# A second copy of the context in 32x32 squares, transposed in place by VectorE, instead of TensorE's context transposes

## What is computed

```python
h = _lin(_layernorm(x), hW, hb);  c = _lin(ctx_1024, cW, cb)
q = _lin(h, qW, qb);  k = _lin(c, kW, kb);  v = _lin(c, vW, vb)
attn = softmax(einsum('bqf,bkf->bqk', q, k) * scale)      # 512 queries x 8192 keys, per batch
x = x + _lin(einsum('bqk,bkf->bqf', attn, v) + q, oW, ob)
x = x + ssm_layer(_layernorm(x))      # layernorm, in_w, convolution with a 16-term kernel, silu gate, out_w
x = x + chosen_expert(_layernorm(x))  # argmax of 8 gates, one 512x512 matrix per token
```

## Time and profile before

| what | value |
|---|---|
| median of 3 runs | 1283.13 us (1282.91 to 1284.45) |
| the profiled execution's own time | 1280.48 us |
| its span, first to last instruction | 1278.8 us |
| TensorE matmul busy | 1203.6 us, 94% |
| VectorE busy | 910.0 us, 71% |
| ScalarE busy | 493.8 us, 39% |
| GpSimd busy | 327.9 us, 26% |
| mean granted TensorE clock | 0.977 of full speed |

### The profile page before, as it was taken

The page is one execution under the profiler, slowest core; times in us unless marked ns, Lnnn a source line. Parts: engine busy times, 40 slices in busy tenths (PEclk is TensorE's granted clock), DMA queues, the critical chain, the costliest instruction groups (busy, mean ns, idle before and its releaser), DMA issues.

```text
span 1278.8 us, 17356 instructions
## 1 busy us (share of the span) xinstructions
PE 1203.6 (94%) x5953; PEld 985.3 (77%) x5953; DVE 910.0 (71%) x1847; ACT 493.8 (39%) x1091; POOL 327.9 (26%) x312
## 2 busy tenths in 40 slices
PE   7999999999999999999999999999999999926397
PEld 6787788888888888888788888888888888825275
DVE  7853577777777777775277777777777766797584
ACT  4211244444444444442433333333333352322252
POOL 4613122222111111212122222222222231824234
PEclk9999999999999999999999999999999999968699
DMA  7311010001000100120011011000100010104692
GB/s 259 108 34 33 1 67 34 34 33 66 33 33 33 66 33 33 34 108 1 3 65 34 34 37 61 33 33 35 64 33 33 34 66 34 67 1 173 208 352 105
DMA packets 29054, 81.25 MB, mean 64 GB/s; under 512 B 4383, under 2 KB 4415, under 8 KB 24912
## 3 DMA queue, kind: packets, MB, share of 16 engines
q1 hardware_dynamic: 25648, 70.69, 15.6%
q0 software_dynamic: 3360, 9.97, 2.2%
HBM read 74.35 MB, written 8.13 MB: 65 GB/s over the span
## 4 chain that ended last, share of the span: by engine, by line
PE 85%; DVE 9%; DMA 2%; POOL 1%; ACT 1%; issue 1%; SPq 0%; POOLq 0%; DVEq 0%; ACTq 0%
PE bank L456 38%; PE bank L607 28%; PE bank L464 5%; PE bank L594 4%; PE bank L819 2%; PE bank L691 2%; PE bank L660 2%; DMA zT<-in_L_ffn_expert_w_dram 1%; DVE probs L1301 1%; DMA spectra<-mixed,gather_rows 1%; POOL rows L1797 1%; DMA stage<-in_L_xattn_hW_dram 1%; PE bank L490 1%; DVE bnst L1157 1%; DVE h L1301 0%
## 5 line engine op out<-in xcount | busy, mean ns | idle before, releaser
L938 ACT ACTIVATE probs<-bank,nbias 128x512 f32<-128x512 f32 x128 | 88.1, 688 | 448.7 <-DVE nbias L1364 448.7
L1371 DVE TENSOR_TENSOR probsT<-bank,probsT 128x512 fp32r<-128x512 f32 x128 | 88.5, 692 | 176.3 <-ACT probsT L930 176.2
L607 PE MATMUL bank<-hl_A,probsT 128*128 128x512 f32 x768 | 195.1, 403 | 1.8 <-POOL hl_A L1679 1.8
L607 PE MATMUL bank<-hl_F,probsT 128*128 128x512 f32 x768 | 195.2, 403 | 1.2 <-POOL hl_F L1679 1.2
L456 PE MATMUL bank<-hl_B,hl_D 128*128 128x512 f32 x768 | 192.3, 399 | 0.0
L456 PE MATMUL bank<-hl_C,hl_D 128*128 128x512 f32 x768 | 191.5, 398 | 0.0
L607 PEld LDWEIGHTS bank<-hl_A,probsT 128*128 128x128 f32 x768 | 139.8, 189 | 30.9 <-issue 2.0
L607 PEld LDWEIGHTS bank<-hl_F,probsT 128*128 128x128 f32 x768 | 139.8, 189 | 30.2 <-issue 1.4
L1679 POOL TENSOR_TENSOR hl_F<-stage,hl_F 128x512 fp32r<-128x512 f32 x62 | 80.0, 1291 | 321.2 <-ACT hl_F L921 321.2
L456 PEld LDWEIGHTS bank<-hl_C,hl_D 128*128 128x128 f32 x768 | 140.2, 188 | 27.5
L1679 POOL TENSOR_TENSOR hl_A<-stage,hl_A 128x512 fp32r<-128x512 f32 x62 | 80.1, 1292 | 314.2 <-ACT hl_A L921 314.2
(11 more groups left out here) (386 smaller groups left out, 1750.3 us busy)
## 6 DMA issues: line engine op xcount, KB each, us to landing
stage<-in_ctx_dram SPq DMA_DIRECT2D x32, 1024.0 KB, 4.8
stage<-in_L_ffn_expert_w_dram SPq DMA_DIRECT2D x9, 1024.0 KB, 8.1
stage<-in_L_attn_in_w_dram SPq DMA_DIRECT2D x4, 1024.0 KB, 5.9
zT<-in_L_ffn_expert_w_dram SPq DMA_DIRECT2D x3, 1024.0 KB, 7.6
rows<-in_L_ffn_expert_w_dram SPq DMA_DIRECT2D x3, 1024.0 KB, 6.2
xb<-in_x_dram SPq DMA_DIRECT2D x2, 1024.0 KB, 13.3
spectra<-in_L_attn_in_w_dram SPq DMA_DIRECT2D x2, 1024.0 KB, 5.4
mixed<-xb SPq DMA_DIRECT2D x2, 1024.0 KB, 4.6
```

Of the source, the lines that this page charges most:

```text
L607: last = nc.tensor.matmul(obank[u % 2][:], probsT[u % 2][:, a, j, :], nat[b][par][:, c, j, :], start=(j == 0 and (a, c) == PASSES[0]), sto ...
L938: nc.scalar.activation(probs[u % 2][:], sbank[u % 2][:], ACT.Exp, bias=nbias[:, q:q + 1], scale=SCALE, accum_out=rsum[:, q:q + 1]).then_in ...
L1371: nc.vector.tensor_tensor(probsT[u % 2][:, 1], tbank[u % 2][:].rearrange("p (j q) -> p j q", j=T), probsT[u % 2][:, 0].bitcast(F32), ALU.s ...
```

## The change

One block of the turned context is no longer made by TensorE. Each chunk is loaded a second time by four DMAs (`load_squares`): in DMA j the 128 features 128j to 128j+127 of all 512 rows go to partitions 32j to 32j+31, in pieces of 128 features (512 bytes). VectorE then transposes, in place, 32x32 squares of a view in which every fourth element belongs to a block (`squares`), so that a partition holds one feature. ScalarE copies the high part from this view, and GpSimd instead of VectorE subtracts for the low part. The feature blocks become features 4n+k instead of 128k+n, for which the folded query weights and the first chunk are taken in `block_columns`. The natural load takes rows j*128+p instead of 4p+j.

The buffers for the squares are `yT` and `uT` in batch 0, and the two halves of `xb` (the residual x) in batch 1. So x is written to DRAM (`x_kept`) and read back at the end of `attention(1)`.

```diff
-        sbank, tbank, obank, cbank = bank[0:2], bank[2:4], bank[4:6], bank[6:8]
+        sbank, tbank, obank = bank[0:2], bank[2:4], bank[4:6]
+        square_rows = [[m.rearrange("p t n -> p (t n)").rearrange("p (i w) -> p i w", w=P) for m in pair] for pair in (
+            (yT, uT), (xb[:, 0], xb[:, 1]))]
+        squares = [[m.rearrange("p t n -> p (t n)").rearrange("p (i c m) -> p m i c", c=SQUARE, m=T) for m in pair] for pair in (
+            (yT, uT), (xb[:, 0], xb[:, 1]))]
...
-        ctx_rows = ctx_in.rearrange("b (c p j) d -> (b c) p j d", p=P, j=T)
+        ctx_rows = ctx_in.rearrange("b (c j p) d -> (b c) p j d", p=P, j=T)
+        ctx_squares = ctx_in.rearrange("b (c i a) (j w) -> (b c) j a i w", c=NCH, a=SQUARE, j=T)
...
+                    if c == 3 and b == 0:
+                        put_x(1)
                     if c > 2:
-                        sp.wait_ge(cT_ready, blocks + T * (c - 2))
+                        sp.wait_ge(cT_split, blocks + T * (c - 2))
+                        load_squares(b, c)
                     sp.wait_ge(nat_split, base + T * (c - 1))
                     load(f"chunk{c}@{b}", ctx_rows[b * NCH + c])
 
                 for c in range(2):
-                    sp.wait_ge(cT_ready, blocks + BLOCKS - T + T * c)
+                    if b == 1:
+                        sp.wait_ge(cT_split, blocks + BLOCKS - T + T * c)
+                        sp.dma_start(xb[:, c].rearrange("p t n -> p (t n)"), x_kept[c]).then_inc(x_back[c], 16)
                     sp.wait_ge(nat_split, base + STEPS - T + T * c)
                     load(f"in{c}@{b}", matrix(in_w[c * D:(c + 1) * D]))
+
+            def load_squares(b, c):
+
+                for j in range(T):
+                    sp.dma_start(square_rows[b][c % 2][SQUARE * j:SQUARE * (j + 1)], ctx_squares[b * NCH + c, j]).then_inc(in_squares[c % 2], 16)
+
+            def put_x(b):
+
+                if b == 1:
+                    sp.wait_ge(evacuated, EVAC["qo1.3"])
+                else:
+                    sp.wait_ge(rows_ready, ROWS["norm@0"] + 1)
+                sp.dma_start(x_kept[b], xb[:, b].rearrange("p t n -> p (t n)")).then_inc(x_put[b], 16)
...
+            sp.wait_ge(inbias_ready, 1)
+            for c in (1, 2):
...
+            sp.wait_ge(x_put[1], 16)
+            load_squares(1, 1)
+            put_x(0)
+            sp.wait_ge(x_put[0], 16)
+            load_squares(1, 2)
...
+            def columns(w, k):
+                return w[:, k * P:(k + 1) * P]
...
-                products("qc0.#", hlB, hlA)
+                products("qc0.#", hlB, hlA, block_columns)
...
-                transposes("ctx0T.#@0", stage[0])
+                transposes("ctx0T.#@0", stage[0], block_columns)
...
-                def context_block(t, u):
-
-                    par, dd = (u // T + 1) % 2, u % T
-                    if dd == 0:
-                        pe.wait_ge(in_stage[par], (t + (u // T + 1) // 2) * 16 + load0[par])
-                    wait_pos(pe, cT_split, blocks, t * UN + (u - 1))
-                    turned(cbank[dd % 2], stage[par], dd).then_inc(cT_ready, 1)
-
...
                 def context_block(t, u):
                     par, dd = (u // T + 1) % 2, u % T
                     act.wait_ge(cT_ready, t * UN + (blocks + u + 1))
-                    nc.scalar.activation(ctxT[par][:, 0, dd, :], cbank[dd % 2][:], ACT.Copy).then_inc(cT_hi, 1)
+                    if dd == 0:
+                        wait_pos(act, scores_ready, base, t * UN + u)
+                    nc.scalar.activation(ctxT[par][:, 0, dd, :].rearrange("p (i a) -> p i a", a=SQUARE),
+                                         squares[b][par][:, dd], ACT.Copy).then_inc(cT_hi, 1)
...
                 def context_block(t, u):
                     par, dd = (u // T + 1) % 2, u % T
-                    dve.wait_ge(cT_hi, t * UN + (blocks + u + 1))
-                    nc.vector.tensor_tensor(ctxT[par][:, 1, dd, :], cbank[dd % 2][:], ctxT[par][:, 0, dd, :].bitcast(F32),
-                                            ALU.subtract).then_inc(cT_split, 1)
+                    if dd == 0:
+                        dve.wait_ge(in_squares[par], (t + 1) * (16 * T) + b * 16 * T * (NCH // 2 - 1 + par))
+                    block = squares[b][par][:, dd]
+                    nc.vector.transpose(block, block).then_inc(cT_ready, 1)
...
+                if b == 1:
+                    dve.wait_ge(x_back[1], 16)
...
+                def context_block(t, u):
+                    par, dd = (u // T + 1) % 2, u % T
+                    pool.wait_ge(cT_hi, t * UN + (blocks + u + 1))
+                    nc.gpsimd.tensor_tensor(ctxT[par][:, 1, dd, :].rearrange("p (i a) -> p i a", a=SQUARE),
+                                            squares[b][par][:, dd],
+                                            ctxT[par][:, 0, dd, :].bitcast(F32).rearrange("p (i a) -> p i a", a=SQUARE),
+                                            ALU.subtract).then_inc(cT_split, 1)
+
                 def trip(t, first, last):
                     for u in range(UN):
+                        if not (last and u >= T):
+                            context_block(t, u)
                         if not (last and u + 2 >= UN):
                             natural(t, u)
...
                     pool.wait_ge(in_outb, 16)
+                    pool.wait_ge(x_back[0], 16)
```

More of the change, by code:

```diff
@@ L35 @@
 HALF = S // 2
+SQUARE = 32
 NBANK = 8
@@ L272, in build @@
         cT_ready, cT_hi, cT_split = sem("cT_ready"), sem("cT_hi"), sem("cT_split")
+        in_squares = [sem(f"in_squares{n}") for n in range(2)]
+        x_put, x_back = ([sem(f"{n}{b}") for b in range(B)] for n in ("x_put", "x_back"))
         nat_hi, nat_split = sem("nat_hi"), sem("nat_split")
         pv_ready, sums_updated = sem("pv_ready"), sem("sums_updated")
+        x_kept = nc.dram_tensor("x_kept", [B, P, T * D], F32)
         mixed = nc.dram_tensor("mixed", [TOKENS, 2 * D], F32)
@@ L280, in build, with block_columns @@
         block = ctx.enter_context(nc.Block())
+        def block_columns(w, k):
+            return w.rearrange("p (n m) -> p m n", m=T)[:, k]
         def matrix(w):
@@ L405, in _ @@
             load("chunk0@0", ctx_rows[0])
+            sp.wait_ge(inbias_ready, 1)
+            for c in (1, 2):
+                load_squares(0, c)
             attention_loads(0)
@@ L445, in open_bank, with product @@
                 return bank[BANK[n]]
-            def product(dst, lhs, k, rhs, kept=None, turned_by=None):
+            def columns(w, k):
+                return w[:, k * P:(k + 1) * P]
+            def product(dst, lhs, k, rhs, kept=None, turned_by=None, part=columns):
                 for t in range(T):
@@ L455, in product @@
                     for a, c in PASSES:
-                        last = nc.tensor.matmul(dst, lhs[:, a, t, k * P:(k + 1) * P], rhs[:, c, t, :],
+                        last = nc.tensor.matmul(dst, part(lhs[:, a, t, :], k), rhs[:, c, t, :],
                                                 start=(t == 0 and (a, c) == PASSES[0]),
@@ L459, in product, with turned @@
                 return last
-            def turned(dst, src, k):
+            def turned(dst, src, k, part=columns):
                 for t in range(T):
-                    last = nc.tensor.transpose(dst[:, t * P:(t + 1) * P], src[:, t, k * P:(k + 1) * P], ident[:])
+                    last = nc.tensor.transpose(dst[:, t * P:(t + 1) * P], part(src[:, t, :], k), ident[:])
                 return last
@@ L474, in kept_split_of, with transposes @@
                 pe.wait_ge(kept_split, KEPT[name] + T)
-            def transposes(name, src):
+            def transposes(name, src, part=columns):
                 for k in range(T):
                     job = name.replace("#", str(k))
-                    turned(open_bank(job), src, k).then_inc(filled, 1)
+                    turned(open_bank(job), src, k, part).then_inc(filled, 1)
             def row_transposes(name, src, first):
@@ L491, in turn_rows, with products @@
                 last.then_inc(filled, 1)
-            def products(name, lhs, rhs):
+            def products(name, lhs, rhs, part=columns):
                 for k in range(T):
                     job = name.replace("#", str(k))
-                    product(open_bank(job)[:], lhs, k, rhs).then_inc(filled, 1)
+                    product(open_bank(job)[:], lhs, k, rhs, part=part).then_inc(filled, 1)
             def prepare():
@@ L528, in prepare @@
                 kept_split_of("q1")
-                products("qc1.#", hlB, hlF)
+                products("qc1.#", hlB, hlF, block_columns)
                 evacuated_from("vWT.3")
@@ L617, in trip @@
                     for u in range(UN):
-                        if not (last and u >= T):
-                            context_block(t, u)
                         scores(t, u)
@@ L718, in middle @@
                 pe.wait_ge(in_stage[0], LANDED["chunk0@1"])
-                transposes("ctx0T.#@1", stage[0])
```

(3 more changed lines are left out.)

1 line of the change is left out of this document (removed).

## The result

The changed kernel takes **1334.23 us** by the median of its runs (1329.7 to 1337.5). The kernel before took 1283.22 us in the same session. The ratio is 1.0393, with a 95% interval of 1.0362 to 1.0425, so the change costs 51 us. The forecast was slower by 107 us, 1390. The sign and the range held, the size did not.

A forecast was written before the change was run, and what follows sets the result against it. TensorE and VectorE's loop were taken to be both at the limit in batch 0. Waits of `nbias` added 58 + 49 = 107 us to 1280.5, or 1388; with 2.65 for the median, 1390 us, range 1272 to 1470.

The forecast's parts named there:

- TensorE isn't what the step waits for, and sparing it alone wins nothing: Attention loop: TensorE's 120 x 0.46 = 55 us saving counts only as far as VectorE's loop follows, which it can't.
- the chain of the earlier trace: Work that ended last in the profile before: 85% TensorE, 9% VectorE, inviting the reading that whatever leaves TensorE is won.
- The transpose takes 0.68 us: VectorE, per context block: the transpose replaces a subtraction of 0.68 us, change 0, bounds -7 and +82 us over 120 steps.
- ScalarE's copy takes 0.63 us and GpSimd starts 0.13 us ahead of `nbias`: Each context block: the copy ends at 1.41 us, GpSimd's subtraction starts at 1.49 and `nbias` would start at 1.62.
- nothing meets: Rival, chance 0.13: with a copy of 0.96 us or more GpSimd starts behind `dmax`; 9 us less, 1274.
- `nbias` waits for GpSimd's new subtraction, 0.97 us a step: VectorE's loop: `nbias` held until about 2.80, exponential 0.97 us later; 58 us in batch 0, 49 in batch 1.
- only `dmax` waits: Rival, chance 0.16: GpSimd holds `dmax`, not `nbias`, so `alpha` starts 0.29 us later; 17 plus 8 us, 1309.
- signs of being wrong: Profile after: `nbias` and `dmax` keep their lengths, steps under 6.4 us, or the granted clock falls because TensorE idles.
- GpSimd half again as long: Rival, chance 0.20: GpSimd's new subtraction takes 1.94 us, everything comes 1.62 us later; 185 us more, 1468.
- The hidden edits: Extra chunk loads, stores and loads of x, first squares and strided weight loads: each taken as 0 us.
- TensorE can spare that: First scores of each chunk: the low part comes 2.1 us later than VectorE's did, which TensorE, ahead of VectorE, absorbs.

The follow-up runs named there:

- reordered kernels: Changed kernel and kernel before, each with VectorE's kernel term or output products and `lsum` moved ahead of the turned probabilities' subtraction: 1231.26 and 1282.58 us.
- reordered changed kernel: Changed kernel with VectorE's kernel term or output products and `lsum` moved ahead of the turned probabilities' subtraction: 1231.26 us, 0.9596 of the kernel before.

## Why the prediction was right or wrong

- *TensorE isn't what the step waits for, and sparing it alone wins nothing* held. With VectorE's order unchanged its loop paced every regular step, and the kernel with a transpose of one square shows the 5.98 us behind it. Taken alone, the chain of the earlier trace rows would have promised 55 us. Its price of 0.46 us per context block held to the last digit (6.44 to 5.98, reordered kernels).
- *The transpose takes 0.68 us* failed, and this is the term behind the 51 us. It measured 1.125 us, inside the bounds of 0.62 and 1.36, and the 0.68 is what it needs with neighbouring elements (0.70). The prediction asked of GpSimd's new operand what its step of four elements would cost, did not ask it of VectorE's, which has the same step, and asked it of ScalarE's only in a rival.
- *ScalarE's copy takes 0.63 us and GpSimd starts 0.13 us ahead of `nbias`* failed for the same reason. The copy takes 1.12, and GpSimd starts 0.35 us behind `nbias` and 0.22 behind `dmax` (322.02 against 321.67 and 321.80). The rival *nothing meets* had named this condition, a copy of 0.96 us or more. It held in the regular steps, while that rival's gain did not come, since it too had kept the transpose at 0.68.
- *`nbias` waits for GpSimd's new subtraction, 0.97 us a step,* is the step of the prediction that failed. It carried the whole +107 us. `nbias` kept its 0.21 us in every run. It was drawn from a four-element TENSOR_SCALAR of 1225 ns. `nbias` has one element and is not held 0.18 us behind GpSimd's start, nor in the reordered changed kernel, where 102 of the 128 start inside a GpSimd subtraction and none takes more than 218 ns. `dmax` beside it is held. The rival *only `dmax` waits* had the rule right. Two of the prediction's own signs of being wrong came true: `nbias` and, in most steps, `dmax` kept their lengths, and the granted clock fell where TensorE idled.
- *GpSimd half again as long* did not come true. It takes 1.54 us in place of 1.28, a fifth more.
- The hidden edits held: loads, stores and queues cost nothing that a profile shows. A packet of q1 took 0.06 us (29.5% of 16 x 1335.7 us for 101872), half of the 0.12 that was priced. *TensorE can spare that* was said of a low part that comes 2.1 us later than VectorE's did, and it failed: GpSimd's ends 3.92 us after the context work starts (319.65 to 323.57), 3.24 later than the 0.68 before. TensorE waits 70 us for it in total (36.0 and 34.0), and with the clock behind these waits this made the irregular steps.

Put the measured transpose into the rival *nothing meets*: a regular step is 0.39 us longer (0.42 in the transpose, 0.03 less in `mx`, 0.65 for 0.68). Batch 0 pays 60 x 0.39 = 23.4 us, batch 1 60 x (6.29 + 0.39 - 6.44) = 14.4, together 38. Measured without the clock's part are 38.5 us (1321.85 against 1283.39), and the clock's part, with what follows from it, is the other 12.4. So the forecast had the right loop and the wrong addend. The 107 us came from a wait that no run shows, and the 51 from a transpose priced at 0.68 in place of 1.125 us and from a clock that the sum left out. The direction came out right by another road, and that is luck in part: with `nbias` not held, the prediction's other prices give the 1309 of its first rival, and the meeting with `dmax` that makes this 26 us does not occur in the regular steps either.

## What to carry to other kernels

Before an engine is spared, find the loop over the engines that closes the step, and take the work out of that loop's way first; here the same edit was worth +51 us in one order and -52 in another. Price each moved instruction by its access step on every engine that reads the new layout, not on one of them. And where an engine waits at a seam, look at the granted clock right behind the wait; here 12 matmuls took 1.44 us longer behind a wait of 2.91.

## What the runs showed of the hardware

- 512 float32 per partition, out of SBUF, read at every fourth element (16 bytes) and as neighbours: VectorE's 32x32 transposes in place 1.13 and 0.70 us, ScalarE's copy 1.12 and 0.63, GpSimd's subtraction with one such input 1.54 and 1.28, VectorE's subtraction with one such input 1.08 (with neighbours not run). The Trainium skill, GPSIMD Engine Reference, Performance pitfalls for Q7 kernels, has about half again as many cycles for such a step; for GpSimd these runs have a fifth more, and the measurement decides.
- VectorE beside a GpSimd subtraction: a TENSOR_SCALAR of one element per partition kept its 0.21 us inside 119 subtractions of one kernel, while a TENSOR_TENSOR of one element waited until GpSimd was through (0.88, 1.00 and 1.21 us, for 0.15). A TENSOR_SCALAR of four elements had waited too. What makes the difference between one and four elements was not tried.
- After a wait of 2.9 us TensorE's granted clock was 0.65 over the next 4.4 us, and 12 matmuls took 4.35 us in place of 2.91. With throwaway transposes in that wait it was 1.00, which was worth 12 us over 28 chunk starts.
